# Routed feed-forward of a two-layer block: first product made transposed, unchosen experts masked in PSUM

## The reference, cut to what matters

```python
out_shared = sq_relu(xf @ Ws1) @ Ws2
logits = xf @ Wr                                   # 8 experts
top_vals, top_idx = top_k(logits, 2)
prob = trunc(einsum('tk,tke->te', softmax(top_vals), onehot))
h = sq_relu(einsum('td,edf->tef', xf, W1))         # 8 experts x 64 hidden = 512
y = einsum('tef,efd->ted', h, W2)
out_routed = einsum('ted,te->td', y, prob)
return out_shared + out_routed
```

## Time and profile before

| | |
|---|---|
| median of 3 runs | 1480.84 us (1480.16 to 1483.44) |
| the profiled execution | 1481.03 us |
| its span, first to last instruction | 1479.2 us |
| mean granted TensorE clock | 0.979 |
| PE, DVE, ACT, POOL busy | 95%, 87%, 86%, 58% |
| PEld busy | 65% |

### The profile page before, as it was taken

The page is one execution under the profiler, slowest core; times in us unless marked ns, Lnnn a source line. Parts: engine busy times, 40 slices in busy tenths (PEclk is TensorE's granted clock), DMA queues, the critical chain, the costliest instruction groups (busy, mean ns, idle before and its releaser), DMA issues.

```text
span 1479.2 us, 34876 instructions
## 1 busy us (share of the span) xinstructions
PE 1404.5 (95%) x9748; PEld 963.9 (65%) x9905; DVE 1283.9 (87%) x5266; ACT 1275.8 (86%) x4428; POOL 859.0 (58%) x1345
## 2 busy tenths in 40 slices
PE   4678999999999999999999999999999999999998
PEld 2455666666676666667666666766666676666654
DVE  3677988998998999899899999989999998998886
ACT  3657888899988889998888999888899988889886
POOL 3113656556565656656565565656556565655567
PEclk8689999999999999999999999999999999999999
DMA  4410000000000000000000000000000000000000
GB/s 136 139 56 16 10 14 16 15 15 12 15 11 14 16 15 15 12 15 11 14 16 15 15 13 15 11 14 16 15 15 13 15 11 14 14 15 7 8 3 4
DMA packets 68960, 30.18 MB, mean 20 GB/s; under 512 B 19168, under 2 KB 68768, under 8 KB 68768
## 3 DMA queue, kind: packets, MB, share of 16 engines
q1 hardware_dynamic: 51552, 19.31, 4.9%
q10 hardware_dynamic: 17216, 8.65, 2.1%
HBM read 17.31 MB, written 2.10 MB: 13 GB/s over the span
## 4 chain that ended last, share of the span: by engine, by line
PE 62%; ACT 13%; DVE 11%; POOL 7%; issue 4%; SPq 2%; DMA 1%; POOLq 0%; ACTq 0%; another core or an unknown queue 0%; DVEq 0%
PE psC L309 43%; PE psA L309 7%; PE psB L309 6%; DVE nmA L2240 5%; ACT PTA L1344 3%; ACT PS L1344 3%; POOL accO L3405 3%; DVE PTB L2365 3%; ACT TE L1344 3%; DVE TE L2497 2%; ACT PTB L1344 2%; SPq L3776 2%; PE psA L421 1%; POOL accO L3413 1%; PE psB L553 1%
## 5 line engine op out<-in xcount | busy, mean ns | idle before, releaser
L3405 POOL TENSOR_TENSOR accO<-accO,TE 128x512 f32<-128x512 f32 x192 | 246.3, 1283 | 143.9 <-DVE TE L2497 137.7
L1344 ACT ACTIVATE TE<-psC,gate 128x128 f32<-128x128 f32 x1024 | 300.1, 406 | 17.7 <-PE psC L309 10.4
L1344 ACT ACTIVATE TE<-psC,gateO 128x128 f32<-128x128 f32 x1024 | 292.5, 375 | 24.8 <-PE psC L309 16.2
L2497 DVE SCALAR_TENSOR_TENSOR TE<-psC,gate,TE 128x128 f32<-128x128 f32 x1024 | 284.5, 339 | 29.5 <-PE psC L309 18.4
L2497 DVE SCALAR_TENSOR_TENSOR TE<-psC,gateO,TE 128x128 f32<-128x128 f32 x1024 | 287.1, 341 | 13.2 <-PE psC L309 8.2
L3393 POOL TENSOR_TENSOR TE<-TE 128x256 f32<-128x256 f32 x256 | 192.4, 752 | 164.5 <-DVE TE L2497 160.4
L309 PE MATMUL psC<-Vh,xTh 128*128 128x512 f32 x512 | 263.3, 514 | 2.3 <-ACT PS L1344 1.2
L309 PE MATMUL psC<-Oh,ch 128*128 128x512 f32 x512 | 262.9, 513 | 0.2
L309 PE MATMUL psC<-Oh,cl 128*128 128x512 f32 x512 | 203.0, 396 | 0.0
L309 PE MATMUL psC<-Vh,xTl 128*128 128x512 f32 x512 | 202.5, 396 | 0.0
L309 PE MATMUL psC<-Ol,cb 128*128 128x512 bf16 x452 | 176.2, 390 | 0.0
(11 more groups left out here) (228 smaller groups left out, 3426.7 us busy)
## 6 DMA issues: line engine op xcount, KB each, us to landing
bdB<-Kc SPq DMA_DIRECT2D x384, 16.0 KB
raw<-in_L_ffn_v_w ACTq DMA_DIRECT2D x8, 512.0 KB, 4.5
raw<-in_L_ffn_o_w ACTq DMA_DIRECT2D x8, 512.0 KB, 4.2
x_sb<-in_x SPq DMA_DIRECT2D x32, 64.0 KB, 2.1
ctx_sb<-in_ctx SPq DMA_DIRECT2D x32, 64.0 KB, 2.0
bdA<-Kc SPq DMA_DIRECT2D x128, 8.0 KB
Qb<-Qc SPq DMA_DIRECT2D x128, 8.0 KB
bias_sb<-in_mask_Bx1xSxS_ff SPq DMA_DIRECT2D x32, 64.0 KB, 1.9
```

Source lines behind the costliest of these rows:

```text
L1344: return A.activation(o, i, func, **kw)
L2497: m = V.scalar_tensor_tensor(TE[:, i, e], psC[:, p, e * P:(e + 1) * P], gates[:, e:e + 1], TE[:, i, e], ALU.mult, ALU.add)
L3405: G.tensor_tensor(accO[:], TE[:, slot(b, H1)] if h == 1 else accO[:], TE[:, slot(b, H1 + h)], ALU.add).then_inc(o_fe, 1)
```

## The change

The first product of feed-forward 0 is made with the weights stationary and xTA moving: four products, each with two experts' W1s (128 columns) stationary, so that psA[:, 1, :] holds hidden units on partitions by tokens, in four blocks. They leave their accumulation open. VectorE makes out_p, a bf16 tile of 512 columns that is 1 for each token and hidden unit of an expert that is not chosen. Four products of out_p by barred (a bf16 identity times -1e30) add -1e30 to those places in PSUM; the last one signals a_hid. VectorE then takes max(psA, 0) into hg, now already transposed, and ScalarE squares hg from SBUF into hT. The four transposes and the semaphore a_htr go; a_exp(b, 0) waits for a_hT in its place. One constant (barred) is made on GpSimd.

The second norm of a_* gets tiles of its own (stA2, mvA2, rsA2), so a_stats of the next sequence may stand ahead of a_stats2.

The lists of calls are new on all engines: the same calls, in partly another order, and period(i) begins at another place of the cycle. Some moves on TensorE: selectors() comes first of all; b_proj and a_shared stand between outputs(1, 1) and a_ht; a_ht moves ahead of outputs(1, 0). On VectorE c_norm and a_stats of the next sequence move to the stretch of a_max. On ScalarE weights1() precedes a_ctxt(0). On SP the gate weights are loaded among the first and keys0, queries0, weights_ffn come later; products2 precedes products.

```diff
@@ tiles
+        stA2 = sb("stA2", [P, 6])
+        mvA2 = sb("mvA2", [P, 2])
+        rsA2 = sb("rsA2", [P, 1])
-        sure = sb("sure", [P, 1])
-        prob = sb("prob", [P, E0])
-        hg = PTA[:, 0].rearrange("p t s -> p (t s)").rearrange("p (e f) -> p e f", e=E0)
+        unsure = sb("unsure", [P, 1])
+        out_p = sb("out_p", [P, E0 * F0], BF16)
+        barred = sb("barred", [P, P], BF16)
+        hg = PTA[:, 0]
@@ TensorE, a_route
-                mm(psA[:, 1, :], xTA[:], W1s[:].rearrange("p e f -> p (e f)")).then_inc(a_hid, 1)
+                for n in range(NPAIR):
+                    mm(psA[:, 1, n * P:(n + 1) * P], flat(W1s[:, 2 * n:2 * n + 2]), xTA[:], n == 0, False)
@@ TensorE, a_ht
-                pe.wait_ge(a_gate, 6 * b + 6)
-                hgf = hg.rearrange("p e f -> p (e f)")
+                pe.wait_ge(a_gate, 6 * b + 5)
+                pe.wait_ge(s_const, BARRED)
                 for n in range(NPAIR):
-                    m = T.transpose(psA[:, 1, n * P:(n + 1) * P], hgf[:, n * P:(n + 1) * P], ident)
-                m.then_inc(a_htr, 1)
+                    m = mm(psA[:, 1, n * P:(n + 1) * P], out_p[:, n * P:(n + 1) * P], barred[:], False, n == NPAIR - 1)
+                m.then_inc(a_hid, 1)
@@ ScalarE, a_exp
-                act.wait_ge((a_htr, a_y, a_pv, a_pv)[t], b)
+                act.wait_ge((a_hT, a_y, a_pv, a_pv)[t], b)
@@ ScalarE, a_ht
-                act.wait_ge(a_htr, b + 1)
-                copy(flat(hT), psA[:, 1, :], ACT.Square).then_inc(a_hT, 1)
+                act.wait_ge(a_gate, 6 * b + 6)
+                act.wait_ge(a_y, b)
+                copy(flat(hT), flat(hg), ACT.Square).then_inc(a_hT, 1)
@@ VectorE, a_routed
-                    V.tensor_scalar(sure[:], egap[:], 1.0, 1.0, ALU.add, ALU.is_equal).then_inc(a_gate, 1)
+                    V.tensor_scalar(unsure[:], egap[:], 1.0, 1.0, ALU.add, ALU.not_equal).then_inc(a_gate, 1)
...
-                    V.tensor_scalar(prob[:], lg[:], top8[:, 0:1], sure[:], ALU.is_equal, ALU.mult).then_inc(a_gate, 1)
+                    V.tensor_scalar(out_p[:].rearrange("p (e f) -> p e f", e=E0), along(lg[:], F0), top8[:, 0:1], unsure[:],
+                                    ALU.not_equal, ALU.max).then_inc(a_gate, 1)
...
-                V.scalar_tensor_tensor(hg, psA[:, 1, :].rearrange("p (e f) -> p e f", e=E0), 0.0,
-                                       along(prob[:], F0), ALU.max, ALU.mult).then_inc(a_gate, 1)
+                V.tensor_scalar(flat(hg), psA[:, 1, :], 0.0, None, ALU.max).then_inc(a_gate, 1)
@@ GpSimd, more_constants
+                G.tensor_scalar(barred[:], ident_b[:], MASKED, None, ALU.mult).then_inc(s_const, 1)
@@ TensorE, start()
+                selectors()
                 a_ctxt(0)
                 a_keys(0)
+                b_keys(0)
                 a_xt(0)
-                b_keys(0)
                 a_queries(0)
                 a_values(0)
-                selectors()
                 products()
@@ TensorE, period(i)
                 a_route(i - 1)
-                a_shared(i - 1)
                 c_context(i - 4, 1)
                 outputs(i - 4, 1, 1)
+                b_proj(i - 2)
+                a_shared(i - 1)
+                a_ht(i - 1)
                 outputs(i - 4, 1, 0)
-                a_ht(i - 1)
+                b_values(i - 1)
                 outputs(i - 4, 2, 1)
-                b_values(i - 1)
                 a_ffn(i - 1)
```

More of the change, by code:

```diff
@@ L701, in start @@
                 a_pvs(0)
-                b_values(0)
                 a_ut(0)
@@ L708, in start @@
                 a_shared(0)
+                b_values(0)
                 a_ht(0)
@@ L848, in start @@
                 values(0, 7, 1)
-                b_proj(2)
+                a_x1t(3)
                 values(0, 7, 0)
                 outputs(0, 0, 1)
-                a_x1t(3)
+                a_route(3)
                 outputs(0, 0, 0)
-                a_route(3)
                 c_context(0, 1)
+                outputs(0, 1, 1)
+                b_values(3)
                 a_shared(3)
-                outputs(0, 1, 1)
+                a_ht(3)
                 outputs(0, 1, 0)
-                a_ht(3)
-                b_values(3)
                 outputs(0, 2, 1)
@@ L1794, in start @@
                 c_context(0, 1)
+                outputs(0, 1)
                 a_shared(3, 0)
                 a_shared(3, 1)
-                outputs(0, 1)
                 a_ht(3)
                 outputs(0, 2)
+                c_short(0, 1)
+                b_values(3)
                 a_ctxt(4)
@@ L1926, in start @@
                 outputs(2, 4)
+                b_values(5)
                 a_queries(6)
@@ L2042, in end @@
                 a_ht(B - 1)
+                outputs(B - 4, 1)
                 outputs(B - 4, 2)
@@ L2546, in start @@
                 a_stats2(0, 0)
+                a_stats(1, 2)
                 a_stats2(0, 1)
@@ L2665, in start @@
                 c_choice(0, 10)
+                a_stats(3, 2)
                 a_routed(2, 0)
@@ L2734, in start @@
-                a_stats2(3, 0)
-                c_share(1, 1)
-                a_stats2(3, 1)
-                c_context(0, 0)
-                c_share(1, 2)
-                a_stats2(3, 2)
-                values(0, 6)
-                a_norm2(3)
-                values(0, 7)
-                c_share(1, 3)
-                outputs(0, 0)
+                a_stats(4, 0)
+                c_share(1, 1)
+                c_share(1, 2)
+                a_norm2(3)
+                c_context(0, 0)
+                values(0, 6)
@@ L2745, in start @@
+                values(0, 7)
+                b_keys(3)
                 a_top(3, 0)
-                b_third(2)
+                c_stats(2, 0)
                 a_top(3, 1)
                 a_top(3, 2)
-                a_stats(4, 0)
-                c_stats(2, 0)
+                c_share(1, 3)
                 a_routed(3, 0)
+                outputs(0, 0)
                 a_routed(3, 1)
+                c_context(0, 1)
                 a_routed(3, 2)
-                c_context(0, 1)
                 c_stats(2, 1)
@@ L2862, in start @@
                 b_bias(4, 0)
+                c_share(2, 6)
+                c_norm(3)
+                outputs(1, 6)
                 b_bias(4, 1)
-                outputs(1, 6)
                 b_bias(4, 2)
-                b_bias(4, 3)
                 a_max(5, 0)
                 a_max(5, 1)
+                b_bias(4, 3)
                 c_xl_(3)
@@ L2958, in start @@
-                a_max(6, 3)
-                a_maxt(6, 0)
-                outputs(2, 7)
-                a_maxt(6, 1)
-            def period(i):
-                a_withmax(i - 1)
-                c_products(i - 3, 0)
-                c_choice(i - 3, 0)
-                values(i - 4, 0)
-                c_products(i - 3, 1)
-                c_choice(i - 3, 1)
-                c_max(i - 3, 0)
+            def period(i):
+                outputs(i - 5, 4)
+                b_queries(i - 2)
+                outputs(i - 5, 5)
+                b_bias(i - 2, 0)
+                b_bias(i - 2, 1)
+                outputs(i - 5, 6)
+                c_norm(i - 3)
+                a_max(i - 1, 0)
+                b_bias(i - 2, 2)
+                a_max(i - 1, 1)
+                c_xl_(i - 3)
+                a_stats(i, 0)
+                b_bias(i - 2, 3)
+                outputs(i - 5, 7)
+                a_max(i - 1, 2)
+                a_max(i - 1, 3)
+                a_maxt(i - 1, 0)
+                a_maxt(i - 1, 1)
+                c_choice(i - 3, 0)
+                c_choice(i - 3, 1)
+                a_withmax(i - 1)
@@ L3013, in period @@
                 a_routed(i - 1, 0)
-                c_stats(i - 2, 1)
-                a_routed(i - 1, 1)
-                a_stats(i, 2)
-                c_stats(i - 2, 2)
-                a_routed(i - 1, 2)
-                c_context(i - 4, 1)
-                c_share(i - 3, 2)
-                a_norm(i)
+                c_share(i - 3, 2)
+                a_routed(i - 1, 1)
+                c_context(i - 4, 1)
+                a_routed(i - 1, 2)
+                b_third(i - 2)
+                c_stats(i - 2, 0)
+                c_stats(i - 2, 1)
                 outputs(i - 4, 1)
-                c_norm(i - 2)
                 c_share(i - 3, 3)
```

1232 lines of the change are left out of this document (610 added, 622 removed).

## The result

The changed kernel takes 1520.14 us (median of four runs, 1519.67 to 1522.21) where the kernel before took 1481.5 beside it: ratio 1.0262, 95% interval 1.0245 to 1.028. The forecast was 1470 us, with a range up to 1488; the result lies 32 us above the range.

A forecast was written before the change was run, and what follows sets the result against it. TensorE bounds part of the period, including the routed feed-forward; in about a third all three engines are nearly full. -10.6 (TensorE) - 1 (start) + 0 (VectorE, ScalarE) = -11.6 from 1480.84: 1470 us, range 1457 to 1488.

The forecast's parts named there:

- the start: Filling before the steady periods: earlier k_w load and new orders change the time by -1 us, from -5 to +5.
- rival 5: New orders also remove small waits of each period, 0.3 to 0.5 us, another 10 us: 1455 to 1464; chance 0.15.
- Moving c_norm and a_stats to the stretch of a_max: On VectorE: adds nothing in sum, puts some 0.6 us where it is nearly full; taken as covered, though thinly.
- Cover: 717 to 724 us: VectorE's 0.68 us without work was to hide the routing's added VectorE time.
- its net on VectorE: Relu and out_p added, prob and hg removed: +0.17 us a sequence, between -0.1 and +0.4, covered.
- The narrow first product: On TensorE: four narrow fp32 products take 0.81 us where the wide one takes 0.95, saving 0.14 a sequence.
- rival 4: Narrow first product costs more, weight loads not hidden: 1.54 us for 0.95, net 0.40 more a sequence, 1494; chance 0.03.
- The Trainium skill's rule: Issue spacing of 81 ns for 128 columns, 131 for 512: splitting the first product would add 0.39 us a sequence.
- The barred products, out_p, relu: New masking steps: four bf16 products 0.21 us on TensorE; out_p 0.5 and relu from PSUM 0.65 us on VectorE.
- TensorE's saving: Routed feed-forward on TensorE: 1.35 us becomes 1.02, 0.33 a sequence, 10.6 us if all of it reaches the end.
- Rival 3: Square of hT late behind an expert group, TensorE waits up to 0.8 us in a_ffn: up to 1496; chance 0.20.
- at about the same time: At the start: first scores, which also need Qb, were to come no earlier or later than before.

The follow-up runs named there:

- new_order_old_sums: The changed kernel with its new orders and second statistics tiles, but the old routing (wide first product, prob, hg, four transposes): 1520.27 us, ratio 1.0263.
- before_short_pool: The kernel before with GpSimd's sums of expert results cut to 8 of every 128 columns: 1476.26 us, ratio 0.9966.
- old_order_new_sums: The kernel before with the new routing in the old orders, but for two local moves: 1481.53 us, ratio 0.9998.
- before_more_work: The kernel before with about 2.5 us a sequence of one-source VectorE reductions of a constant added where the changed kernel has its holds: 1547.07 us, ratio 1.0431.
- before_no_first_product: The kernel before with the wide first product cut from 512 to 8 columns, 0.8 us less TensorE work a sequence: 1482.33 us, ratio 1.0004.
- after_one_source: The changed kernel with short two-source or normalizing VectorE operations made one-source tensor_reduce, GpSimd's sums at full length: 1483.68 us, ratio 1.0002.
- after_few_collisions: The changed kernel with six calls of VectorE's period moved away from second place behind a group of four expert passes: 1512.72 us, ratio 1.0214.

## Why the prediction was wrong

**The step that failed.** The new orders had a price only in the start ("from -5 to +5, since the orders of some 300 calls per engine are new") and as a gain in rival 5. For the period I counted the moved calls as covered: "Moving c_norm and a_stats to the stretch of a_max adds nothing in sum". The orders gave VectorE 2.3 us a sequence more (new_order_old_sums), nearly all of it holding, and the period became 44.42 us, 1.30 more, where I forecast 42.8. I summed an operation's duration as if it were a property of the operation. The trace of before had the warning: best<-best,gsum on 16 columns took a mean of 332 ns where x<-x_sb,ob on 128 took 294, and its single instructions take from 0.16 to 1.27 us, so some were held already (with short sums, in before_short_pool, the mean is 241). I did not read GpSimd's rows beside VectorE's.

**Cover.** I took VectorE's 0.68 us without work in 717 to 724 us for room. That cover was enough for the routing: its net on VectorE is +0.37 us a sequence in old_order_new_sums, inside my -0.1 to +0.4, and costs nothing. It says nothing of other parts of the period: there 2.3 us more in the changed kernel cost 38 us in all, and the 2.5 us of before_more_work, with the holds that they made, 64.

**The narrow first product.** Forecast 0.81 us from a_ffn's form, measured 0.98; it costs 0.03 more than the wide one where I counted 0.14 less. The sign of rival 4 was right, its size (0.59) was not. The Trainium skill's rule that I set against it ("TensorE: Matmul & The Clock Gate", Back-to-back issue gap) has the right sign; the +0.39 us estimated from its figures is thirteen times too large here.

**The barred products, out_p, relu.** 0.21 forecast, 0.20 measured; 0.5 and 0.546; 0.65 and 0.69. Right. **W2s** I left at 0.81; it is 0.91 in old_order_new_sums. In the changed kernel it takes 0.89 (695.87 to 696.76).

**TensorE's saving.** 0.33 us a sequence forecast, 0.07 there; and before_no_first_product shows that even 0.8 us at this place would have brought nothing. That the 10.6 us count in full ("if all of it reaches the end"), because the chain lies on TensorE there, was the second wrong step. It cost the 10 us of forecast gain.

**Rival 3** had the right side and 0.20 of the chance, but not the cause, and its 1496 us is 24 short: the Square is not late by a group (W2s is at 5.38 after a_route, 0.14 later than before), and the exposure of c_norm and a_stats was put at 0.6 us of work, not at holds of calls that were always there.

**The start.** k_w's product was to come 3 to 4 us earlier; the start of the changed kernel, against the earlier trace rows:

```profile
14.63 3.79 PE L313 MATMUL psC<-raw 128*128 128x128 f32 x16 [3.62 <-DMA raw<-in_L_ffn_q_w]
...
23.31 0.58 PE L313 MATMUL psA<-bdA,Qb 128*128 128x512 bf16 x1 [4.90 <-issue]
...
41.91 0.59 PE L313 MATMUL psA<-Wrs,xTA 128*128 128x8 f32 x2 [0.37 <-ACT xTA L1349]
```

A product of that group is 2.6 us earlier, but the first scores, which need Qb, are at 23.31 where they were at 20.92, and the first a_route at 41.91 where it was at 39.20. My "at about the same time" was 2.4 us off. after_one_source has this start too and ends at 1483.68, so by that run the start is no more than some 2 us of the loss.

## What to carry to other kernels

When a change moves calls about, read VectorE's and GpSimd's rows side by side: the same short operation takes 0.22 us just ahead of a GpSimd sum and 0.78 just behind its start, and a group whose mean duration doubles at equal shape is the sign. Put a tensor_reduce, or an operation that reads PSUM, into the slots behind the operation that releases such a sum (a tensor_scalar of one source can be held too), and reprice every call that an order moves, not only the calls that a change adds. Before a saving on the bounding engine is counted, ask what the next thing there waits for: 0.8 us cut ahead of a wait for other engines' steps was worth nothing, 0.93 us cut elsewhere a third.

## What the runs showed of the hardware

A VectorE instruction with two sources in SBUF that starts while GpSimd runs a tensor_tensor from SBUF lasts until that one ends: 0.22 us becomes 0.78 beside a sum of 0.73 (MtA), 0.16 becomes 1.25 beside one of 1.31 (best<-best,gsum). GpSimd's sums keep their length: accO<-accO,TE has a mean of 1291 ns in the changed kernel and 1283 before. tensor_scalar on fp32 in SBUF is held as well, with one tensor source: xnA 0.34 to 0.70 us, gp<-gp 0.21 to 0.68, gsum<-gsum,rs 0.20 to a mean of 0.56 in after_few_collisions. Where both begin within 0.05 us the recorded starts do not tell which gets in: in the kernel before, gsum<-best, of two sources, begins at 754.52 beside a sum that began at 754.48, takes its 0.16 us, and the sum takes 0.80 where others take 0.73.

Operations that read PSUM are not held: in the changed kernel nmA takes its 0.68 us with 1.2 us of a sum still to run, and x<-psA,x (one source in PSUM, one in SBUF) its 0.29 with 1.1. tensor_reduce from SBUF is not held either: the reductions in place of the held ones took 0.15 to 0.29 us beside full sums. out_p, a tensor_scalar with a broadcast input, took 0.546 us in all runs that have it, but no sum ran beside it in the periods looked at, so these runs do not say whether it can be held.

The Trainium skill says the same of the port pair that the two engines share: page "SBUF — State Buffer", sections "SBUF: two separate sides" and "Who interferes with whom": an exclusive lock for the whole instruction, taken by a VectorE operation in a two-port mode or with two SBUF inputs (only against a GpSimd operation that reads SBUF), or by a GpSimd operation, whichever starts first. The traces agree where the sum starts first, with the numbers above. Its price here was 38 us of 1482, for about seven held instructions a sequence.
